# VectorE's mixed stage with its independent chains laid into each other

## The reference

```python
rank = jnp.cumsum(ni, axis=-1) - ni
nb = ni.sum(-1)                                  # neighbours of a node
skip = jnp.where(nb > T, (nb + K - 1) // K, 1)   # T, K = 10, 2
rem = neigh & (sk > 1) & (rank % sk == sk - 1) & mask[:, :, None]
rem = rem | jnp.swapaxes(rem, 1, 2)              # edges taken away, both ways
...
s = jnp.sort(jnp.where(nd[..., None], x[:, None, :, :], jnp.inf), axis=2)
for tau, w in zip((0.25, 0.5, 0.75), (0.25, 0.5, 0.25)):
    pos = tau * jnp.maximum(nv - 1, 0)           # nv: neighbours that are left
    lo, hi = floor(pos), ceil(pos)
    agg = agg + w * (v_lo + frac * (v_hi - v_lo))  # s at lo and at hi
out = x + agg
y = (relu(out @ W1 + b1) @ W2 + b2) * mask
```

## Time and profile before

| | us |
|---|---|
| median of 3 runs | 3187.29 |
| lowest and highest | 3184.47 and 3189.19 |
| the profiled execution | 3195.59 |
| its span | 3193.8 |

### The profile page before, as it was taken

One profiled execution on the slowest core, in us unless ns is written; L12 is line 12 of the kernel. 1 busy time (PEld: TensorE's weight loads), 2 busy tenths in 40 slices (PEclk: granted clock), 3 DMA queues, 4 the chain that ended last, 5 costly groups with the idle time before them and its releaser, 6 DMA issues.

```text
span 3193.8 us, 45583 instructions
## 1 busy us (share of the span) xinstructions
PE 2251.2 (70%) x16081; PEld 1000.7 (31%) x16234; DVE 2805.5 (88%) x5398; ACT 1991.7 (62%) x3077; POOL 12.4 (0%) x24
## 2 busy tenths in 40 slices
PE   0000014387888988888888988888898889776996
PEld 0000002232333333333333333333333333224674
DVE  7999998998999989899999999999898999545776
ACT  2111443278787887778788877878788877741322
POOL 0000000000000000000000000000000000000000
PEclk6555557688998989899999989899898989886777
DMA  3001000000101001010100101010100100000101
GB/s 68 0 0 26 31 0 0 22 24 11 37 8 34 13 29 33 10 33 12 36 11 31 21 21 33 12 37 9 32 15 27 34 10 19 10 20 27 40 26 40
DMA packets 126915, 72.05 MB, mean 23 GB/s; under 512 B 95512, under 2 KB 110058, under 8 KB 126698
## 3 DMA queue, kind: packets, MB, share of 16 engines
q1 hardware_dynamic: 122570, 68.23, 8.3%
q10 hardware_dynamic: 4128, 1.05, 0.2%
HBM read 41.05 MB, written 15.58 MB: 18 GB/s over the span
## 4 chain that ended last, share of the span: by engine, by line
PE 44%; DVE 32%; ACT 13%; issue 7%; SPq 2%; DMA 1%; DVEq 0%; ACTq 0%
PE ring L624 10%; PE rows L665 8%; ACT hot L1078 6%; PE bcast L637 5%; PE found_bank L677 5%; DVE keys L1326 3%; DVE keys L1327 3%; PE bcast L748 2%; PE bcast L757 2%; PE bank L919 2%; ACT prod L1071 2%; DVE picked L1524 2%; DVE delta L1367 2%; DVE delta L1365 1%; DVE perm L1369 1%
## 5 line engine op out<-in xcount | busy, mean ns | idle before, releaser
L1078 ACT ACTIVATE hot<-bcast,consts 128x1024 f16<-128x1024 f32 x744 | 830.7, 1117 | 136.0 <-PE bcast L637 135.5
L665 PE MATMUL rows<-hot,table 128*64 128x512 f16 x3072 | 525.7, 423 | 0.0
L624 PE MATMUL ring<-member,neigh_t 128*128 128x512 bf16 x1925 | 488.9, 392 | 40.0 <-issue 15.1
L1071 ACT ACTIVATE prod<-rows 128x512 f32<-128x512 f32 x720 | 431.1, 599 | 10.4 <-PE rows L665 10.4
L637 PE MATMUL bcast<-idx_t,consts 32*128 32x512 f16 x1488 | 311.3, 415 | 159.6 <-ACT hot L1078 158.0
L654 PE MATMUL rows<-fine_rows,consts 32*128 32x512 bf16 x768 | 316.3, 412 | 18.8 <-DMA fine_rows<-turned 18.1
L562 PE MATMUL ring<-identb,adj_b 128*128 128x128 bf16 x256 | 33.1, 258 | 368.9 <-ACT adj_b L974 357.6
L624 PEld LDWEIGHTS ring<-member,neigh_t 128*128 128x128 bf16 x2048 | 187.4, 101 | 318.8 <-issue 100.2
L677 PE MATMUL found_bank<-prod,consts 128*32 128x512 f32 x1536 | 240.2, 702 | 11.3 <-ACT prod L1071 10.5
L637 PEld LDWEIGHTS bcast<-idx_t,consts 32*128 32x128 f16 x1488 | 70.8, 92 | 499.0 <-ACT hot L1078 332.2
L1524 DVE TENSOR_TENSOR picked<-picked 128x3072 uint16<-128x3072 uint16 (+2 forms) x192 | 209.5, 1091 | 11.2
(11 more groups left out here) (347 smaller groups left out, 4326.8 us busy)
## 6 DMA issues: line engine op xcount, KB each, us to landing
late<-in_adj_dram SPq DMA_DIRECT2D x16, 1024.0 KB, 5.4
adjt_d<-neigh_t SPq DMA_DIRECT2D x16, 512.0 KB, 2.7
fine_rows<-turned SPq DMA_DIRECT2D x512, 8.0 KB
fine_rows<-turned SPq DMA_DIRECT2D x512, 16.0 KB
turned<-adjt_d SPq DMA_DIRECT2D x16, 512.0 KB, 3.5
adj_s<-adjt_d SPq DMA_DIRECT2D x16, 512.0 KB, 3.8
xt_d<-keys SPq DMA_DIRECT2D x2, 1024.0 KB, 10.5
parts_d<-parts SPq DMA_DIRECT2D x4, 512.0 KB, 6.9
```

Of the source, the lines that this page charges most:

```text
L624: ins = mm(ring[u % 2][:, :], kept_t[:, j, P * i:P * i + P], member[:, j, n // 2, 512 * (n % 2):512 * (n % 2) + 512], start=(j == 0), stop ...
L665: ins = mm(rows[u % 2][C * h:C * h + C, :], table[:, s, GROUPS * h + g8, :], hot[:, u % HOT, h, :], start=False, stop=(s == 1), skip_group ...
L1071: run(prod[:, u % DEEP, :], rows[u % 2][:, :], ACT.Relu).then_inc(S["prod_by_act"], 1)
L1078: run(hot[:, u % HOT].rearrange(flat), spread_bank(l, u)[0][:, 0:2, :].rearrange(flat), ACT.Relu, bias=eq_bias[:, :]).then_inc(S["hot_read ...
```

## The change

PE, ACT, SP and GpSimd are untouched. On DVE `region` is replaced by `ahead` (as long as there is a graph whose bits are searched) and `behind` (the last two). The chains other than the search become generators, with a `yield` behind each instruction. The new helper `beside(ins, other)` issues an instruction of the search, then one instruction of the other chain, and only then waits for the first. `alone(other)` runs a generator to its end. Inside the generators each instruction waits for its own producer by number. `tell` is replaced there by a wait on that producer and the signal. `degree`, the sum of rows for the graph convolution, is taken out of `gcn_start` and put ahead of `ffn_end`. The calls of `units` that did nothing are gone from `select` and `ahead`.

```diff
+            def beside(ins, other):
+                n = did(ins)
+                next(other, None)
+                need(n)
+            def alone(other):
+                for _ in other:
+                    pass
...
-                did(ts(step, bit, 0.0, None, ALU.is_equal))
-                then(tt(r, r, t, ALU.subtract))
-                then(ts(t.bitcast(I16), bit, -1.0, None, ALU.mult))
+                stays = did(ts(step, bit, 0.0, None, ALU.is_equal))
+                beside(tt(r, r, t, ALU.subtract), other)
+                flags = did(ts(t.bitcast(I16), bit, -1.0, None, ALU.mult))
...
             def gcn_start(l):
+                v.engine_nop().then_inc(S["z_ready"], 1)
                 dve.wait_ge(S["sd_ready"], 3 * l + 1)
-                norm_b(pre)
-                tell("x1_ready")
-                then(ts(small[:, 12, :], rowsum[:, l, :], 1.0, None, ALU.add))
-                did(ts(small[:, 11, :], small[:, 12, :], 0.0, None, ALU.is_gt))
-                then(ts(small[:, 13, :], small[:, 12, :], 1e-30, None, ALU.max))
-                tell("z_ready")
+                yield from norm_b(pre)
+                v.engine_nop().then_inc(S["x1_ready"], 1)
                 dve.wait_ge(S["sd_ready"], 3 * l + 2)
...
-            def region(t_of, p, l, d):
+            def ahead(t_of, p, l, d):
+                first = chain(rank_bits(p), members(p, 0)) if p is not None else pause(10)
+                ffn = chain(degree(d), ffn_end(d)) if d is not None else nothing
+                start = chain(pause(1), gcn_start(d)) if d is not None else nothing
+                need(count[0])
+                dve.wait_ge(S["sums_ev"], 2 * (NT * t_of + NT))
+                other = chain(first, ffn)
+                bits_start(t_of, other)
+                bits_first(other)
+                alone(other)
+                pop(wl, x2, x4, x8, t, start)
+                if p is not None:
+                    clear_own(p)
+                alone(start)
+                other = chain(pause(1), members(p, 1)) if p is not None else nothing
+                bits_second(other)
+                if p is not None:
+                    middle = middles(p)
+                    narrow(x4, 4, middle)
+                    alone(middle)
+                    alone(other)
...
+                other = gcn_middle(d) if d is not None else nothing
+                narrow(x2, 2, other)
+                alone(other)
+                if p is not None:
+                    drop(p, 0)
+                    alone(members(p, 2))
+                    drop(p, 1)
+                    other = members(p, 3)
+                    bits_last(other)
+                    drop(p, 2)
+                    alone(other)
+                    drop(p, 3)
+                    for j in range(NT):
+                        keep(p, j)
+                    other = chain(pause(2), limits(p))
...
+                ending = chain(gcn_end(d), pause(2), gcn_done(d)) if d is not None else nothing
+                other = chain(other, ending)
+                bits_next(t_of, other)
+                tell("idx_ready")
+                alone(other)
+                restart()
+            def behind(l, d):
```

More of the change, by code:

```diff
@@ L8 @@
 from contextlib import ExitStack
+from itertools import chain
 import concourse.bass as bass
@@ L1267, in then, with pause @@
                 need(did(ins))
+            def beside(ins, other):
[5 more added lines that the diff above has]
+                    pass
+            def pause(n):
+                for _ in range(n):
+                    yield
+            nothing = iter(())
             def restart():
@@ L1614, in bits_last, with bits_second @@
-            def bits_last():
-                then(tt(t, wl, sh, ALU.logical_shift_right))
-                then(ts(t, t, 1, None, ALU.bitwise_and))
-                then(tt(bit, r, t, ALU.is_ge))
-                then(tt(pos, sh, bit, ALU.add))
+                beside(tt(wl, wl, t, ALU.bitwise_xor), other)
+            def bits_second(other):
+                beside(ts(t, x8, 255, None, ALU.bitwise_and), other)
+                beside(tt(bit, r, t, ALU.is_ge), other)
+                kept = did(tt(t, t, bit, ALU.mult))
+                beside(ts(sh, bit, 3, None, ALU.logical_shift_left), other)
+                need(kept)
+                beside(tt(r, r, t, ALU.subtract), other)
@@ new lines, in narrow @@
+            def narrow(field, size, other):
+                beside(tt(t, field, sh, ALU.logical_shift_right), other)
+                beside(ts(t, t, 2 ** size - 1, None, ALU.bitwise_and), other)
+                beside(tt(bit, r, t, ALU.is_ge), other)
+                kept = did(tt(t, t, bit, ALU.mult))
+                beside(ts(bit, bit, size // 2, None, ALU.logical_shift_left), other)
+                need(kept)
+                did(tt(r, r, t, ALU.subtract))
+                beside(tt(sh, sh, bit, ALU.add), other)
@@ L1675, in ffn_end @@
+                need(last)
             def ffn_end(l):
                 dve.wait_ge(S["y_ps"], l + 1)
+                made = [0] * NT
                 for i in range(NT):
-                    did(stt(out=pre[:, i, :], in0=dense_bank[:, C * i:C * i + C], scalar=mask_t[:, i, l:l + 1], in1=x_all[:, i, l, :], op0=ALU.mult, op1=ALU.add))
-                need(count[0])
-                norm_a()
+                    made[i] = did(stt(out=pre[:, i, :], in0=dense_bank[:, C * i:C * i + C], scalar=mask_t[:, i, l:l + 1], in1=x_all[:, i, l, :],
+                                      op0=ALU.mult, op1=ALU.add))
+                    yield
@@ L1682, in gcn_start, with degree @@
+                yield from norm_a(made)
+            def degree(l):
+                one_more = did(ts(small[:, 12, :], rowsum[:, l, :], 1.0, None, ALU.add))
+                yield
+                need(one_more)
+                did(ts(small[:, 11, :], small[:, 12, :], 0.0, None, ALU.is_gt))
+                yield
+                last = did(ts(small[:, 13, :], small[:, 12, :], 1e-30, None, ALU.max))
+                yield
+                need(last)
             def gcn_start(l):
+                v.engine_nop().then_inc(S["z_ready"], 1)
@@ L1718, in region @@
-            def region(t_of, p, l, d):
-                units(l, STEP[0])
-                if t_of is not None:
-                    need(count[0])
-                    dve.wait_ge(S["sums_ev"], 2 * (NT * t_of + NT))
-                    bits_start(t_of)
-                units(l, STEP[1])
-                if p is not None:
-                    members(p, 0)
-                units(l, STEP[2])
-                if t_of is not None:
-                    bits_first(l)
-                units(l, STEP[3])
-                if d is not None:
-                    ffn_end(d)
-                units(l, STEP[4])
-                if t_of is not None:
-                    pop(wl, x2, x4, x8, t)
+                yield from norm_b(xb(l))
@@ L1767, in region @@
-                if t_of is not None:
-                    narrow(x2, 2)
-                units(l, STEP[11])
-                if p is not None:
-                    keep(p, 2)
-                    keep(p, 3)
-                    members(p, 3)
-                    limits(p)
-                units(l, STEP[12])
-                if t_of is not None:
-                    bits_last()
-                if d is not None:
-                    gcn_end(d)
-                units(l, STEP[13])
-                if t_of is not None:
-                    bits_next(t_of, l)
-                    tell("idx_ready")
+                    for j in range(NT):
+                        keep(p, j)
@@ new lines, in ahead @@
+                    other = chain(pause(2), limits(p))
+                else:
+                    bits_last(nothing)
+                    other = nothing
+                ending = chain(gcn_end(d), pause(2), gcn_done(d)) if d is not None else nothing
[5 more added lines that the diff above has]
+            def behind(l, d):
+                units(l, STEP[3])
+                alone(degree(d))
+                alone(ffn_end(d))
+                units(l, STEP[5])
+                alone(gcn_start(d))
+                units(l, STEP[7])
+                alone(gcn_middle(d))
+                units(l, STEP[12])
+                alone(gcn_end(d))
```

338 lines of the change are left out of this document (188 added, 150 removed).

## The result

The changed kernel takes 3357.87 us (median of 4 runs, 3353.33 to 3369.15); the kernel before took 3186.37 us on the same comparison (4 runs, 3184.47 to 3189.19). The ratio is 1.053, 95% interval 1.0513 to 1.0547: slower by 5.3%, as forecast (3376 us, 3300 to 3450). The profiled execution took 3353.33 us, span 3351.5, against 3195.59 and 3193.8. Across groups the ratios are the fair measure, not the medians.

The account below looks back on a forecast made before the run. Bound: a balanced pipeline, where it counts when VectorE's signals leave. Thirteen periods +157, preparation only +6, first region -3, together +160; clock +29; from 3195.6 to 3385 us profiled, less 8.3 for the median: 3376 us, range 3300 to 3450.

Parts of the forecast that it names:

- rival four: Interleaving shortens no VectorE step; each costs 0.12 us more, 6 + 5 us per period, 3490 us; chance 0.03.
- rival one: VectorE paces the kernel and its savings come through: 3142 us; chance 0.05.
- Step 1: Second `pop`, with `gcn_start` laid in and waiting for ScalarE's roots: `clear_own` starts 0.8 us later.
- Step 2: Cleared diagonal to `middle_ready`: 9.2 us with the search's steps between, so ScalarE's `apart_of` is 2.7 us late.
- Step 3: From `middle_ready` to the last drop: TensorE's `both_ways` moves 6.5 us late and TensorE stands still for 4.6 us.
- Step 4: `both_ways` to the count of the kept: count comes at 1761.0, `limits` starts at 1761.5, VectorE idles some 4 us.
- Step 5: Count of the kept to `idx_ready`, `bits_next` interleaved: 11.7 us instead of 19.2, winning 7.5 us.
- Step 6: `gcn_end` behind `idx_ready`: third `z_ready` at 1775.2 instead of 1760.95 us, ScalarE's third root waits 6.9 us more.
- Step 7: Third root to `turn_idx` on TensorE and ScalarE: 11.3 us instead of 12.5, so `turn_idx` starts 12.1 us late.
- Rival two: Only the third root delays, `both_ways` stays put: `turn_idx` 5.6 us late, 3260 us; chance 0.12.
- Rival three: TensorE's clock runs at half speed more than allowed for, above all behind the root: 3467 us; chance 0.12.
- Rival five: Gains and losses cancel within 0.2%; chance 0.02.

Follow-up runs that it names:

- experiment seven: Changed kernel reordered so VectorE's signals come first, plus four more 128x1536 multiplications of 0.98 us in `bits_next`: 3172.09 us, 0.989 of the kernel before.
- experiment five: Changed kernel's order, but every `beside` waits before and behind the laid-in instruction, so no wait is covered: 3514.66 us, 1.0993 of the kernel before.
- experiment two: Changed kernel with `middles`, drops early again, nothing laid into `narrow` or `bits_next`, `gcn_end` still behind `idx_ready`: 3319.64 us, 1.0385 of the kernel before.
- experiment three: Changed kernel with `middles`, drops and `gcn_end` early again, nothing laid into `narrow` or `bits_next`, other interleaving kept: 3166.31 us, 0.9908 of the kernel before.
- experiment six: Kernel before, nothing interleaved, with only `gcn_end` moved from ahead of `bits_next` to behind `idx_ready`: 3350.39 us, 1.0471 of the kernel before.
- experiment one: Changed kernel with only `gcn_end` and its third `z_ready` put back ahead of `bits_next`, drops still late: 3282.03 us, 1.0269 of the kernel before.

## Why the prediction was right, and where it was not

*What bounds the kernel.* Right. VectorE with 88% busy was no bottleneck but the source of signals: with 86.7 us less of its busy time the kernel is 5.3% slower, and four extra instructions per graph in experiment seven changed nothing that can be told.

*The cost of a wait*, 0.12 us: right, as the rows of experiment five show, though it is not the whole of that version's loss. So rival four (no step gets shorter, 3490 us) falls; so does rival one (VectorE paces, 3142 us), its condition, a third `z_ready` that comes in time, being met in no period of the change.

*Step 1* (diagonal 0.8 us late): 0.6 by the medians. Right.

*Step 2* (9.2 us from the cleared diagonal to `middle_ready`, `apart_of` 2.7 late): 9.1, and 1813.27 - 77.63 - 1732.99 = 2.65 in this period; 1.7 by the medians of all, from 99.3 to 101.0. Right for the period worked on, one microsecond too much for the 13.

*Step 3* (last drop 6.5 us late, TensorE idle 4.6): 5.5 late by the medians; in the period worked on, 1828.00 - 77.63 = 1750.4 against a forecast of 1750.5. TensorE idles 3.6 there and 51.4/14 = 3.7 on average: 0.9 less than thought. The wait is the right one.

*Step 4* (count at 1761.5, VectorE idles some 4 us): 1839.27 - 77.63 = 1761.6, and 3.68 us. Right.

*Step 5* (11.7 us to `idx_ready`): 11.5. Right; this is the saving that the change is after, and it is real.

*Step 6* (root waits 6.9 us more): 6.42 in this period, 79.1/13 = 6.1 on average. Right, and experiments two, three and six show that this is the move that costs, whatever the rest of the order.

*Step 7* failed in its size: 11.3 us from the root to `turn_idx`, because TensorE would have got ahead in its wait. It took 13.2. The rows above show why: TensorE was busy for 1.45 of 4 us ahead of 1850.2, then ran 7 us at 0.52 of its clock, so at 1.2 GHz, and 8 products that take 1.90 us at 1.00 took 3.59. Before, the same stretch ran at 1.00. The head start is there, with 56 products left in the stretch instead of 68. In experiment one, where the root doesn't wait, the stretch takes 12.3 us at 1.00 in all 13 periods. The forecast counted the clock as a general term and the head start here; the head start was eaten by the clock.

*The sum.* Forecast +160, +29 for the clock, +189 together; measured +157.7 between the spans. Term by term: the 13 periods 157 + 29 = 186 against 160.0; preparation only, +6 against +4.0; first region, -3 against -1.6; the rest, 0 against -4.7. So the mis-sized term is that of the 13 periods, by 2.0 us in each. The working took the period of 139.8 us at 0.93 as the kernel before and added a loss of clock only to the change: 139.8 + 12.1 + 2.2 = 154.1 per period, which is exactly the mean measured. That it is exact is partly luck: the general 2.2 us for the clock cover what step 7 lacked, 1.9 us. But the mean before was 141.8, since some of its periods already lost time as the one of 145.70 in the earlier trace rows did: the base was 2.0 us too low, 26 us in 13 periods. By TensorE's busy time for the same products (1594.84 to 1616.51) the clock cost 22 us more in the change, against the 29 of the forecast. The bound of +60, where each of the two new standstills is charged by the Trainium skill's rule that idling halves the clock ("TensorE: Matmul & The Clock Gate", section "Part 1: The HAM clock gate"), was nearly three times the measured amount, though the fall to 0.52 behind a mostly idle stretch agrees with it in kind.

*The signs named in advance* all came: 79.1 us for the third root against some 90, 51.4 for the drops against 55, the indices 15 us ahead of `turn_idx` against 13, periods of 153.6 us, VectorE at 81%.

*Rival two* (only the third root delays, 3260 us) was right in that this wait decides, wrong in that `both_ways` stays put. Its price was not tested as it stands, with `both_ways` in place and a shortened `bits_next`; experiment two, its nearest test, came out at 3319.64 us without anything laid into `bits_next`. *Rival three* (the clock, 3467 us): no. *Rival five* (it cancels): no; it gains only with both signals early, as experiment three shows.

*What stays open.* Experiment three should have been level with before (3187 us forecast, 3165 to 3205) and is 27 us faster than the kernel before timed beside it. Its trace against that of before: 6 us up to the end of the first region, 3 in the next period, 17 in the 13 periods, 4 behind. In the 13 periods TensorE's busy time for the same products fell by as much, 1594.84 to the 1576.62 us of this row:

```profile
776.70:2602.30 1825.60, 1576.62 (x11519) 642.81 (x11648) 1645.87 (x3445) 1470.66 (x2316) 0.00 (x0) 0.92 0.09 24
```

So these 17 us go with TensorE's clock and not with VectorE's 54 us of saved busy time. Two signals do leave earlier in three: the second `z_ready`, for which ScalarE's second root waited 29.9 us in 13 graphs before and waits in none of these periods, and x1, for which TensorE waited 10.4 us in 13 graphs before and doesn't wait in these periods. `both_ways` starts at 109.5 us instead of 110.6. Which of these small gaps lets the clock hold was not tried.

## What to carry to other kernels

In a pipeline whose engines wait for each other, an interleaving is judged by when each signal leaves, not by the work that it saves: first list the signals that another engine is waiting for today or reaches within a few microseconds, and lay nothing ahead of them. Here laying chains into each other gave +5.3% with two signals behind them and -1.2% with the signals first and fewer chains laid in, and one moved call was worth 4.7%. Two delays of one order overlap when both end in the same wait, so price them together, and take the base from the mean over the periods rather than from the cleanest one.

## What the runs showed of the hardware

A wait of VectorE for its own previous instruction costs 0.12 us where nothing covers it: 0.39 against 0.28 us from start to start in the earlier trace rows, and 0.25 us for two such waits in experiment five. In this kernel a stall costs TensorE twice: in the change a wait of 5.70 us was followed by 8 products in 3.59 us instead of 1.90. What I had not expected is how exactly the periods repeat: ten of the change's 13 and nine of experiment six's are within 0.1 us of 153.6 us, and in nine of the change's ten the granted clock falls to half in the same five places of the period, within 0.2 us. Experiment three alternates between 139.0 and 140.9 us, while the kernel before wandered between 139.4 and 145.7.
